# A decoder layer on one core: five engines' programs written out in full, and the FFN weight set-up rearranged

## What is computed

```
x = layernorm(x + rwkv(x))            # token shift, K/V/R projections, a recurrence over the tokens, Wo
x = layernorm(x + cross_attention(x)) # 16 heads of 16, 77 context rows, RMS norm, rotary, softmax, Wo
x = layernorm(x + ffn(x))             # 256 -> 1024 -> 256, ternary weights, 8-bit activations
```

```
scale = 1 / clip(mean(abs(w)), 1e-5)
wq = clip(round(w * scale), -1, 1) / scale
```

## Time and profile before

| | |
|---|---|
| median of 3 runs | 1227.24 us |
| lowest and highest | 1225.63 and 1232.81 us |
| the profiled execution | 1232.12 us |
| its span, first to last instruction | 1230.3 us |
| mean granted TensorE clock in it | 0.955 of full speed |

### The profile page before, as it was taken

One profiled execution on the slowest core, in us unless ns is written; L12 is line 12 of the kernel. 1 busy time (PEld: TensorE's weight loads), 2 busy tenths in 40 slices (PEclk: granted clock), 3 DMA queues, 4 the chain that ended last, 5 costly groups with the idle time before them and its releaser, 6 DMA issues. The chain is left out here.

```text
span 1230.3 us, 22947 instructions
## 1 busy us (share of the span) xinstructions
PE 1087.0 (88%) x6466; PEld 814.7 (66%) x6466; DVE 1027.3 (84%) x2447; ACT 866.3 (70%) x1581; POOL 542.6 (44%) x1142
## 2 busy tenths in 40 slices
PE   1648999999999899989999999989999999998774
PEld 1436677777777677767777677767777677766651
DVE  3678899999999799999999899989999899986442
ACT  0344777787788677777788677777788677776544
POOL 4255454544444455444444455444444455443200
PEclk9877999999999999999999999999999999998785
DMA  6000011111110111111110111111110111100000
GB/s 212 18 17 9 23 24 31 31 31 32 32 33 11 26 32 31 32 32 31 32 32 8 29 32 31 32 32 31 32 32 9 28 32 31 32 14 11 12 9 18
DMA packets 83117, 37.07 MB, mean 30 GB/s; under 512 B 54838, under 2 KB 82486, under 8 KB 82998
## 3 DMA queue, kind: packets, MB, share of 16 engines
q1 hardware_dynamic: 82997, 35.56, 11.0%
HBM read 24.62 MB, written 8.39 MB: 27 GB/s over the span
## 5 line engine op out<-in xcount | busy, mean ns | idle before, releaser
L895 PE MATMUL pb<-q_t,k_blk 128*128 128x256 f32 (+1 forms) x640 | 186.1, 393 | 1.9 <-ACT p_t L692 1.5
L906 PEld LDWEIGHTS pb<-v_blk,p_t 128*128 128x128 f32 (+1 forms) x1280 | 153.6, 198 | 11.0 <-ACT p_t L692 5.6
L906 PE MATMUL pb<-v_blk,p_t 128*128 128x34 f32 (+2 forms) x1280 | 157.4, 281 | 2.1 <-ACT p_t L692 2.1
L666 ACT ACTIVATE gate_silu<-pg,gate_scale 128x512 f32<-128x512 f32 x128 | 88.2, 689 | 99.9 <-PE pu L941 99.9
L499 POOL TENSOR_TENSOR mneg<-zeros,mv 128x2 f32<-128x2 f32 x96 | 18.9, 197 | 306.6 <-DVE mv L1076 306.6
L895 PEld LDWEIGHTS pb<-q_t,k_blk 128*128 128x128 f32 (+1 forms) x640 | 102.5, 191 | 43.5 <-ACT p_t L692 8.3
L692 ACT ACTIVATE p_t<-pb 128x512 f32<-128x512 f32 (+1 forms) x160 | 95.3, 596 | 49.6 <-PE pb L896 49.2
L1268 DVE TENSOR_REDUCE m_pad<-pb 128x4 bf16<-128x308 f32 x256 | 117.4, 469 | 5.0 <-PE pb L876 4.9
L1084 DVE SCALAR_TENSOR_TENSOR mix<-dx,vec,x_t 128x256 f32<-128x256 f32 x192 | 108.8, 607 | 8.9 <-POOL dx L562 8.9
L1206 DVE TENSOR_TENSOR hid<-gate_silu,pu 128x512 f32<-128x512 f32 x128 | 87.6, 684 | 20.6 <-ACT gate_silu L666 17.2
L569 POOL TENSOR_TENSOR den_cur<-e_cur,bb 128x512 f32<-128x512 f32 x32 | 37.8, 1182 | 141.9 <-DVE bb L1140 141.9
(11 more groups left out here) (174 smaller groups left out, 2828.0 us busy)
## 6 DMA issues: line engine op xcount, KB each, us to landing
x_t<-xt SPq DMA_DIRECT2D x32, 256.0 KB, 2.8
x_tok<-x SPq DMA_DIRECT2D x32, 256.0 KB, 3.1
out<-outb SPq DMA_DIRECT2D x32, 256.0 KB, 3.2
ctx_t<-ctxt SPq DMA_DIRECT2D x32, 77.0 KB, 3.0
w_sb<-wts SPq DMA_DIRECT2D x8, 256.0 KB, 4.9
v_blk<-v_sb SPq DMA_DIRECT2D x128, 9.6 KB
hid<-wg SPq DMA_DIRECT2D x1, 1024.0 KB, 7.3
hid_int<-wu SPq DMA_DIRECT2D x1, 1024.0 KB, 9.4
```

Of the source, the lines that this page charges most:

```text
L666: sc.activation(gate_silu[:, u % 2, :], pg[:, :], ACT.Silu, scale=gate_scale[:, u // 2:u // 2 + 1]).then_inc(sil_ready, 1)
L895: mm(dst, k_blk[p][:, g, cols], q_t[p][:, g, :], start=True, stop=False)
L906: last = mm(pb[j][:, c0:c0 + NHEAD[n] * VW], p_t[0:k, q, s, j * P:(j + 1) * P], v_blk[p][0:k, g, n, 0:NHEAD[n] * VW], start=q == 0 and s == 0,
```

## The change

All five programs are written out in full: the hardware loop becomes a Python loop, so steps 8 to 31 are straight code too, and their semaphore values and addresses are constants. The loads of wg, wu, wd move ahead of the five projection weights. The absolute sums move to ACT's `warm(1)` as three Abs activations with accumulated output; their element output goes to the bf16 weight tiles and is overwritten later. PE's sum over partitions moves to `warm(1)`. The scales and the three scale-and-round passes stand together in DVE's `warm(2)`. The subtraction of the constant becomes three Copy activations with a bias in ACT's `warm(3)`, which write bf16. Both clips become one pass on DVE over bf16, in `warm(4)`, three in all.

```diff
@@ schedule
-            with eng.Fori(first // PAIRS_A_LOOP, LAST // PAIRS_A_LOOP) as n:
+            for n in range(first // PAIRS_A_LOOP, LAST // PAIRS_A_LOOP):
@@ SP
             sp.dma_start(ctx_t[0][:, :, :], ctx_v[0]).then_inc(ctx_loaded[0], 16)
+            for n, (w, t) in enumerate(((wg, G), (wu, G), (wd, INNER // P))):
+                sp.dma_start(stages[n].rearrange("p (t n) -> p t n", t=t),
+                             w.rearrange("(t p) n -> p t n", p=P)).then_inc(stage_loaded[n], 16)
             for n in (WO, XQ, XK, XV, XO):
                 load_weight(n, w_loaded)
...
-            for n, (w, t) in enumerate(((wg, G), (wu, G), (wd, INNER // P))):
-                sp.dma_start(stages[n].rearrange("p (t n) -> p t n", t=t),
-                             w.rearrange("(t p) n -> p t n", p=P)).then_inc(stage_loaded[n], 16)
@@ ACT
+            def weight_sums():
+                for n in range(3):
+                    act.wait_ge(stage_loaded[n], 16)
+                    sc.activation(quantised[n], stages[n], ACT.Abs, accum_out=wsum[:, n:n + 1]).then_inc(abs_ready, 1)
+
+            def weight_integers():
+                for k, n in enumerate((2, 1, 0)):
+                    act.wait_ge(round_ready, k + 1)
+                    sc.activation(quantised[n], stages[n], ACT.Copy, bias=-MAGIC).then_inc(int_ready, 1)
+
             def warm(i):
                 if i == 1:
                     act.wait_ge(pool_setup, 3)
+                    weight_sums()
+                if i == 3:
+                    weight_integers()
@@ PE
                 if i == 1:
                     pe.wait_ge(pool_setup, 4)
                     pe.wait_ge(w_loaded, 16 * 5)
-                if i == 2:
-                    pe.wait_ge(dve_setup, 1)
+                    pe.wait_ge(abs_ready, 3)
                     mm(pt[:, 0:3], ones[:, :], wsum[:, :], start=True, stop=True).then_inc(sums_ready, 1)
@@ DVE
-            def weight_integers(n, k):
+            def weight_rounded(n):
                 v.tensor_scalar(stages[n], stages[n], winv[:, n:n + 1], MAGIC, ALU.mult, ALU.add).then_inc(round_ready, 1)
-                dve.wait_ge(round_ready, 2 * k + 1)
-                v.tensor_scalar(stages[n], stages[n], MAGIC, 1.0, ALU.subtract, ALU.min).then_inc(round_ready, 1)
-                dve.wait_ge(round_ready, 2 * k + 2)
-                v.tensor_scalar((wg_q, wu_q, wd_q)[n][:, :, :].rearrange("p t n -> p (t n)"), stages[n], -1.0, None, ALU.max
-                                ).then_inc(dve_setup, 1)
+
+            def weight_clipped(k, n):
+                dve.wait_ge(int_ready, k + 1)
+                v.tensor_scalar(quantised[n], quantised[n], -1.0, 1.0, ALU.max, ALU.min).then_inc(dve_setup, 1)
...
             def warm(i):
-                if i == 1:
-                    weight_sums()
-                if i == 3:
+                if i == 2:
                     weight_scales()
-                    weight_integers(2, 0)
+                    for n in (2, 1, 0):
+                        weight_rounded(n)
                 if i == 4:
-                    weight_integers(1, 1)
-                    weight_integers(0, 2)
-                if i == 5:
-                    dve.wait_ge(dve_setup, 6)
+                    for k, n in enumerate((2, 1, 0)):
+                        weight_clipped(k, n)
```

More of the change, by code:

```diff
@@ L185, in build @@
         hq_t = sb("hq_t", [P, 2, 8, P], bf16)
+        quantised = [w[:, :, :].rearrange("p t n -> p (t n)") for w in (wg_q, wu_q, wd_q)]
         stages = [hid[:, :, :].rearrange("p j n -> p (j n)"), hid_int[:, :, :].rearrange("p j n -> p (j n)"),
@@ L205, in build @@
         act_setup = sem("act_setup")
+        abs_ready = sem("abs_ready")
         sums_ready = sem("sums_ready")
+        int_ready = sem("int_ready")
         x_loaded = [sem(f"x_loaded{i}") for i in range(2)]
@@ L934, in gate_up @@
                     if isinstance(b, int) and b == 0:
-                        pe.wait_ge(dve_setup, 6)
+                        pe.wait_ge(dve_setup, 5)
                     pe.wait_ge(xqts_ready, b + 1)
@@ L1028, in _ @@
             dve.wait_ge(consts_ready, 1)
[L1030 to L1035, removed]
             def weight_scales():
@@ L1039, in weight_scales @@
                 v.tensor_scalar(wmean[:, :], pt[:, 0:3], 1.0 / (C * INNER), 1e-5, ALU.mult, ALU.max).then_inc(dve_setup, 1)
-                dve.wait_ge(dve_setup, 2)
+                dve.wait_ge(dve_setup, 1)
                 v.tensor_scalar(wd127[:, :], wmean[:, :], 1.0 / 127.0, None, ALU.mult)
                 v.reciprocal(winv[:, :], wmean[:, :]).then_inc(dve_setup, 1)
-                dve.wait_ge(dve_setup, 3)
-            def weight_integers(n, k):
+                dve.wait_ge(dve_setup, 2)
+            def weight_rounded(n):
                 v.tensor_scalar(stages[n], stages[n], winv[:, n:n + 1], MAGIC, ALU.mult, ALU.add).then_inc(round_ready, 1)
-                dve.wait_ge(round_ready, 2 * k + 1)
-                v.tensor_scalar(stages[n], stages[n], MAGIC, 1.0, ALU.subtract, ALU.min).then_inc(round_ready, 1)
-                dve.wait_ge(round_ready, 2 * k + 2)
-                v.tensor_scalar((wg_q, wu_q, wd_q)[n][:, :, :].rearrange("p t n -> p (t n)"), stages[n], -1.0, None, ALU.max
-                                ).then_inc(dve_setup, 1)
+            def weight_clipped(k, n):
+                dve.wait_ge(int_ready, k + 1)
+                v.tensor_scalar(quantised[n], quantised[n], -1.0, 1.0, ALU.max, ALU.min).then_inc(dve_setup, 1)
             def warm(i):
-                if i == 1:
-                    weight_sums()
-                if i == 3:
+                if i == 2:
                     weight_scales()
-                    weight_integers(2, 0)
+                    for n in (2, 1, 0):
+                        weight_rounded(n)
                 if i == 4:
-                    weight_integers(1, 1)
-                    weight_integers(0, 2)
-                if i == 5:
-                    dve.wait_ge(dve_setup, 6)
+                    for k, n in enumerate((2, 1, 0)):
+                        weight_clipped(k, n)
             def ln_stats(i, b):
```

## The result

The changed kernel takes 1196.83 us in the median of 6 runs (1195.89 to 1203.13). Six runs of the kernel before on the same chip gave 1229.1 us (1225.63 to 1232.81). The ratio is 0.9751, with a 95% interval of 0.9719 to 0.9782. The forecast was 1202.0 us.

What follows compares the result with a forecast made beforehand. PE bounds the steady state, with DVE close behind. Loop 21.5, step 2 2.0, step 3 2.9 and ACT's Copies -1.2 sum to 25.2 us; 1227.2 less that is 1202.0 us, range 1190 to 1211.

Steps and rivals of the forecast that it cites:

- A: The forecast itself: the loop's cost goes in full and the start gives 3.7 us, 1202.0 us; chance 0.62.
- B: DVE alone sets the start, so all its passes count: 11.8 us saved there, 1193.9 us; chance 0.17.
- The loop written out: Steps 8 to 28 run at the straight pace of 33.57 us: 21.5 us saved, bounds 12 to 25.
- Rival D: The loop's loss is only in part the branches: 12 us go there, 1211.5 us; chance 0.06.
- Rival E: Straight code must be fetched throughout and stalls an engine in each step, slower at 1252 us; chance 0.03.
- Sums on ACT: At the start, three ACT passes of 2.1 us end at 24.6, with 9 us of cover before DVE wants them.
- a sign of being wrong: PE waiting at the start for a projection weight or for the sums would show the forecast wrong.
- DMA order and tables: At the start, small transfers land by 26.3 us, making tables late; batch 1's dx is ready at 32.5, formerly 39.1.
- Step 2, the scales and rounding: DVE's step 2 begins 6.6 us earlier and gives 5.1 back: 2.0 us gained, up to 3.
- Step 3: On DVE about 5.1 us of passes go, but POOL's qrs holds q_scaled: 2.9 us gained, at least 2.3.
- ACT's Copies: In ACT's step 3, three Copies of 1.87 us delay m_t; with clips of 1.2 each, net 1.2 us lost.
- The subtraction on ACT or on DVE: By the skill's rule, moving it to ACT loses 2.0 us a weight, but only where ACT is late.

Runs made afterwards that it cites:

- e1: The kernel before with only the hardware loop written out as straight code; 1205.15 us, ratio 0.9811.
- e8: The kernel before with two steps instead of four in a pass of the hardware loop; 1207.27 us, ratio 0.9814.
- e4: The changed kernel with batch 1's inputs and the eight small table transfers issued ahead of all FFN and projection weights; 1193.42 us, ratio 0.9730.
- e5: The changed kernel with ACT's three Copies moved from the head of step 3 to the gap in step 2; 1198.33 us, ratio 0.9769.
- e6: The changed kernel with the moves of e4 and e5 together; 1192.30 us, ratio 0.9720.
- e7: The changed kernel with the subtraction back on DVE in step 3, the clip still apart; 1202.78 us, ratio 0.9802.
- e10: e6 with PE's sum ahead of its wait for the projection weights and the clips behind DVE's query pieces; 1193.52 us, ratio 0.9719.
- e12: The changed kernel with seven extra matmuls at the start of step 5, their results thrown away; 1204.09 us, ratio 0.9798.
- e2: The changed kernel with the hardware loop kept, so only the weight set-up differs from the kernel before; 1225.44 us, ratio 0.9955.
- e3: The kernel before with eight steps instead of four in a pass of the hardware loop; 1222.39 us, ratio 0.9924.

## Why the prediction was right, and where it was not

The time lay 5.2 us under the forecast and within the range, and the mechanism of the likeliest case (A) came: the loop's cost went in full, and the start gave less than DVE's passes alone would have (B). The size was worse than that reads. The medians differ by 32.3 us where 25.2 were forecast. 1.9 of these 7 us are hidden in the time, since the six runs of the kernel before stand at 1229.1 and the forecast began from the 1227.2 of three. By the time alone, 1196.83 is nearer B's 1193.9 than A's 1202.0, and the changed kernel run again (1199.74) is nearer A's. It is the parts that decide for A. The 25.2 of the sum stand against 35.8 in the two profiles: 21.8 for the loop's 21.5, 8.1 for the start's 3.7, and 5.8 in the drain, which the sum did not have. That the time fell into the range owes something to the range's width.

**The loop written out: right, and its parts too.** 21.5 us were forecast, 21.8 came in the profile, and e1 showed 21.8 for this edit alone. The steps are 33.55 us in the mean, the pace of the earlier trace rows. The parts can now be read from the kernel before. The five turns lengthened the steps around them by 5.0, 3.1, 4.9, 3.4 and 4.7 us, the larger three with a spell at the lower clock behind them. Without the clock that is 3.2 us a turn, where the prediction's lower bound had 2.4: PE's slack took back hardly any of the branch. The clock added 1.6 on three of the five, where up to 1.7 was forecast for each. Rival D, 12 us only, is out.

What the sum left open was what in a taken branch costs the 3.4 us. I had it as a price of the branch. e8 shows that it is the fetch of a target that is no longer held: eleven branches cost 1.9 us in all, registers included.

**Rival E: did not come.** In straight code nothing waits for instructions in the steps: they take 33.55 us each, as the paces of steps 5 to 7 had it.

**Sums on ACT: right.** The passes took 1.9 us each (forecast 2.1) and ended at 23.1 (forecast 24.6). PE did wait for them, 8.73 us, which the prediction had named a sign of being wrong. But its next work, the projections of batch 1, waited for DVE's mix of 31.15 all the same, so this wait was hidden.

**DMA order and tables: right in kind.** Tables landed for 24.77 (forecast: between 24.8 and 26.3), dx was ready at 31.1 and not 32.5. The mix of batch 1 began at 31.15. I took the later bound, since the queue's end of 26.3 was a safe one. e4 shows that this wait was the path: 10 us earlier tables bring 4.1 us.

**Step 2, the scales and rounding: undersized.** I took 5.1 us for scales and rounding from rows in which a wait stands between each pass and the next. Here they took 0.47 + 3.6. The step gained 42.10 - 38.19 = 3.9 us at its end (`den` of batch 0), where I took 2.0 and had named 3 as the bound.

**Step 3: right.** `den` of batch 1 stands at 67.46 for 73.77, 6.3 us in all, so the step itself gave 2.4 (forecast 2.9).

**ACT's Copies: right in mechanism, wrong in the sign of the term.** They took 1.91 us each (forecast 1.87), and `m_t` held PE for 3.54 us; e5 and e6 put what they cost at 2 to 3 us. But the step did not lose the forecast 1.2: `den` of batch 2 gained 6.8 in all, 0.5 more, and that of batch 3, 8.1. Two terms were off. The clips took 0.68 each and not 1.2. And where PE waited, it had less of the lower clock: before, 13.7 us from 108.7; now 3.4 from 93.4 and 3.4 from 110.4. PE's transposes of q came at 105.26 and not at 109.42 as in the earlier trace rows. The other profiles agree: in the last part of the start, from 89 us on, the old start has 10.2 to 13.7 us at the lower level (four profiles) and the new one 6.8 to 10.2 (six). Where the Copies do not stand there (e5, e6, e7, e10) it is 3.4 to 6.8, so it was not PE's wait for them that brought this. My sum had PE's wait in the path and no term for the clock there. Other profiles of the same start put this in proportion: with the new one the x1 copy of step 7 was at 255.3, 255.7, 257.1 and 258.4, with the old one at 262.9 to 264.7. The gain of the start is 6.6 us between the means (257.0, taking in e12's start at 258.6, and 263.6), against the 3.7 of the forecast.

**The subtraction on ACT or on DVE.** e7 gave it a run: the start is the same within 1 us either way, less than profiles of one start differ by. The Trainium skill, "ScalarE: Activation LUTs", section "Rules for kernel authors", speaks for VectorE; here that choice costs nothing and gives nothing. The about 1990 ns for 2048 elements in the section "What ACT_TABLE_LOAD costs" of the same page of the Trainium skill are near the 1.91 us measured.

**The drain: not in the sum.** I took 0 for it, as its code is the same. It gave 5.8 us in the profile, with 13.7 us less at the lower level, which by the 0.42 above come to 5.7 (estimate). That is the largest miss of a term, ahead of the start's 2.9 to 4.4, and I know of no row of the kernel before that tells its sign. In the medians it can't be parted off. The mean granted clock came to 0.959, just short of the 0.96 that the prediction named as a sign.

**Open.** What decides where the spells at the lower level fall, in the start and in the drain, is not settled. e12 was to shift them, and the start before it moved as well. Work that would hold the level up through the drain was not tried.

## What to carry to other kernels

A hardware loop is dear when its body is too long to stay fetched, not because it branches. Here five turns of a body of four steps lost 21.8 us and eleven turns of a body of two lost 1.9, so before writing a loop out look at the branch's own length and at the bytes of the instruction queues, and try a shorter body. Where set-up work competes with a pipeline's first steps, order the DMA queue by who waits first: the eight small transfers and the inputs of batch 1 in front took another 4 us off a start from which the whole rearrangement had taken between 6 and 8.

## What was not expected of the hardware

- Issuing five projection weights took SP 7.23 us when they stood behind 3 MB of FFN weights (8.37 in e4, where they do too), and 2.76 when they stood ahead. SP of the changed kernel, then of the one before:

```profile
6.00 7.23 SPq L360 DMA_DIRECT2D w_sb<-wts  x5
```

```profile
4.31 2.76 SPq L357 DMA_DIRECT2D w_sb<-wts  x5
```

  Everything behind them in SP's queue, the small transfers too, was issued that much later, until 21.1 us. My sum had only counted bytes.
- Reading the accumulator of an ACT pass is an instruction of its own, of 0.19 us (19.14).
- The POOL pass that runs beside DVE's three pure bf16 passes is held up: 3.48 us for 77x256 elements (0.72 in the earlier trace rows, 1.56 beside float32 passes in e10), 3.10 for 128x32 (0.26 in e10). POOL's spans are rough, but the passes behind it start that much later too.
- The lower clock level can come behind the entry of a loop, where no branch was taken yet (e2 and e3, some 2 us). In both PE had just waited 1.0 to 1.1 us for POOL's `kr`; the kernel before waited 0.51 there and had no spell.
